# A fused attention and feed-forward layer: latent keys on another engine, and the order of both ends

## The reference

```python
qkv = x @ qkv_w + qkv_b                        # 16 heads of 16
local = windowed_attention(q, k, v)            # each token sees the 128 in front of it
pooled = x.reshape(B, 64, 8, D).mean(axis=2)   # 64 latent tokens
rq = x @ rq_w + rq_b                           # 4 latent heads of 16
rk, rv = split(pooled @ rkv_w + rkv_b)
remote = softmax(mask(rq @ rk.T / 4)) @ rv @ rout_w + rout_b
gate = sigmoid(local @ gl_w + remote @ gr_w)   # per head
x1 = layernorm(x + (gate * local + (1 - gate) * remote) @ out_w + out_b)
h = gelu(ternary(w_up) applied to rmsnorm(x1)) # 256 -> 1024
out = layernorm(x1 + ternary(w_down) applied to rmsnorm(h))
```

## Time and profile before

| | us |
|---|---|
| median of 3 runs (lowest, highest) | 1197.87 (1192.1, 1199.39) |
| the profiled execution: its time | 1195.67 |
| its span, first to last instruction | 1193.9 |
| TensorE busy | 1035.2 (87%) |
| VectorE busy | 930.8 (78%) |
| ScalarE busy | 681.3 (57%) |
| GpSimd busy | 714.8 (60%) |
| TensorE's mean granted clock | 0.965 of full |

### The profile page before, as it was taken

One profiled execution on the slowest core, in us unless ns is written; L12 is line 12 of the kernel. 1 busy time (PEld: TensorE's weight loads), 2 busy tenths in 40 slices (PEclk: granted clock), 3 DMA queues, 4 the chain that ended last, 5 costly groups with the idle time before them and its releaser, 6 DMA issues.

```text
span 1193.9 us, 38039 instructions
## 1 busy us (share of the span) xinstructions
PE 1035.2 (87%) x15776; PEld 661.3 (55%) x15776; DVE 930.8 (78%) x2148; ACT 681.3 (57%) x1043; POOL 714.8 (60%) x890
## 2 busy tenths in 40 slices
PE   4767899898999999898999989898999989896855
PEld 2435556565656556565656656565655556563533
DVE  5567888889887878879788878888887887975545
ACT  3414566565656566565656566665646656563733
POOL 5406556675656566675665656675655567564744
PEclk9977999999999999999999999999999999996977
DMA  6640241606133250605233160604225060511000
GB/s 219 177 130 3 79 119 41 176 23 166 50 109 91 74 143 32 185 23 145 54 114 103 49 169 32 178 29 126 74 80 137 32 186 23 150 29 39 2 19 18
DMA packets 51272, 108.19 MB, mean 91 GB/s; under 512 B 8054, under 2 KB 35190, under 8 KB 47990
## 3 DMA queue, kind: packets, MB, share of 16 engines
q1 hardware_dynamic: 50460, 105.75, 31.5%
q10 hardware_dynamic: 640, 0.00, 0.0%
HBM read 71.55 MB, written 34.08 MB: 88 GB/s over the span
## 4 chain that ended last, share of the span: by engine, by line
PE 46%; DVE 34%; ACT 8%; issue 6%; POOL 5%; ACTq 0%; DVEq 0%; POOLq 0%
PE oacc L1508 7%; PE oacc L1489 7%; PE work L1565 6%; PE work L1432 5%; PE scores L1469 4%; ACT Pt L793 4%; DVE Pt L979 3%; PE work L1499 3%; DVE nmax L1059 3%; DVE stats L1146 2%; DVE Pt L1017 2%; DVE x L1122 2%; DVE ytok L1140 2%; PE scores L1411 2%; POOL h_lo L664 2%
## 5 line engine op out<-in xcount | busy, mean ns | idle before, releaser
L793 ACT ACTIVATE Pt<-scores 128x1024 f32<-128x1024 f32 (+1 forms) x256 | 228.7, 915 | 116.3 <-PE oacc L1489 75.2
L1059 DVE TENSOR_REDUCE nmax<-work 128x3 f32<-128x480 f32 x352 | 218.2, 637 | 29.5 <-PE work L1437 24.2
L664 POOL TENSOR_TENSOR h_lo<-hbuf,h_hi 128x512 f16<-128x512 f32 x128 | 149.2, 1170 | 133.8 <-DVE h_hi L1181 133.8
L636 POOL TENSOR_SCALAR_AFFINE_SELECT Pt<-Pt 128x512 f32<-128x512 f32 x256 | 166.1, 649 | 95.0 <-ACT Pt L793 93.8
L628 POOL TENSOR_TENSOR parts<-Pt,parts 128x512 bf16<-128x512 f32 x64 | 72.4, 1159 | 142.7 <-ACT parts L743 133.0
L1432 PE MATMUL work<-Ks,Qs 98*32 98x160 bf16 x4096 | 142.0, 236 | 15.2 <-DVE nmax L1059 11.5
L1489 PE MATMUL oacc<-Pt,Vp 128*32 128x256 f32 (+1 forms) x2048 | 149.2, 358 | 4.0 <-POOL Pt L640 3.6
L1508 PE MATMUL oacc<-wdn_t,h_hi 128*128 128x256 f16 x512 | 118.1, 273 | 17.4 <-POOL h_lo L664 17.4
L1469 PE MATMUL scores<-Qs,Ks 100*32 100x160 bf16 (+4 forms) x4096 | 113.9, 228 | 18.9 <-ACT Pt L793 15.9
L640 POOL TENSOR_SCALAR_AFFINE_SELECT Pt<-Pt 128x512 f32<-128x512 f32 x192 | 126.7, 660 | 0.0
L829 ACT ACTIVATE hbuf<-work 128x512 f32<-128x512 f32 x128 | 76.2, 595 | 76.7 <-PE work L1565 61.4
(11 more groups left out here) (169 smaller groups left out, 2078.1 us busy)
## 6 DMA issues: line engine op xcount, KB each, us to landing
parts_scratch<-parts SPq DMA_DIRECT2D x96, 256.0 KB, 5.6
Qs<-parts_scratch SPq DMA_DIRECT2D x96, 256.0 KB, 5.0
Ks<-parts_scratch SPq DMA_DIRECT2D x96, 256.0 KB, 4.7
xtok<-L_attn_x SPq DMA_DIRECT2D x16, 512.0 KB, 6.8
xres<-L_attn_x SPq DMA_DIRECT2D x16, 512.0 KB, 7.7
y<-ytok SPq DMA_DIRECT2D x16, 512.0 KB, 3.3
nat<-L_ffn_w_up SPq DMA_DIRECT2D x1, 1024.0 KB, 8.3
nat<-L_ffn_w_down SPq DMA_DIRECT2D x1, 1024.0 KB, 10.3
```

The costliest lines, as they stand in the source:

```text
L636: ins = pool.affine_select(out=pt[:, :, 0:P], in_=pt[:, :, 0:P], compare_op=ALU.is_gt, fill=0.0, base=0, pattern=[[0, 4], [1, P]], channel ...
L664: pool.tensor_tensor(h_lo[:, t % NR, :], hbuf[:, t % 2, :], h_hi[:, t % NR, :], ALU.subtract).then_inc(h_lo_ready, 1)
L793: nc.scalar.activation(Pt[:, u % NPT, :, 0:w], scores[:, slot, :, :].rearrange("p k (h q) -> p (k h) q", h=2)[:, :, 0:w], ACT.Exp, scale=S ...
L1059: nc.vector.tensor_reduce(nmax[:, :, :].rearrange("p b h -> p (b h)")[:, first:first + n], work[:, slot, 0:n * BAND].rearrange("p (h c) -> ...
```

## The change

Eight edits, all in the order of the work or in who does it; the result is the same function.

1. In LAT_RKV ScalarE makes `rqT` and, by four instructions with a scale and a bias for each partition (`lat_fold`), the four blocks of `lat_bd` straight from the accumulator. VectorE's two instructions (`rqT`, `rk_sb`) and GpSimd's product go. VectorE now waits for ScalarE's blocks (`bd_ready`) ahead of `rv_bd`. `lat_fold` is made once (step FOLD).
2. GpSimd's fourth subtraction moves from QK+3 to LAT_RKV, which is behind its OUT, for sequences 2 and on.
3. LAT_NORM moves behind the first step UP.
4. Prologue: FOLD (with ScalarE's share of PREP) goes ahead of QK+3, LAT_SCORES and LAT_EXP of sequence 0 ahead of VALUES, `prepare` behind LAT_RKV; GpSimd's EDGES waits for the fourth subtraction.
5. Prologue, beside the tiles A of sequence 0: LAT_SCORES and LAT_EXP of sequence 1 move in among them, VALUES+2 and VALUES+3 behind them.
6. The first ternary matrix (step TERNARY, both passes) moves into the prologue, ahead of LAT_T of sequence 1.
7. The second one is cut into three pieces at u = 2, 5 and 8, and the intermediate result lies in the target itself.
8. The first three score tiles of sequence 15, with their exponentials, move into the second half of sequence 14, behind GATE; TensorE's wait for the maxima moves to the first score tile. GpSimd's masks stay where they were.

```diff
@@ -75,7 +75,7 @@
     ("F", NORM + 1), ("P", LAT_EXP), ("P", VALUES + 1), ("F", XN_T), ("F", XN_T + 1), ("F", XN_HI),
-    ("P", LAT_EXP + 1), ("F", XN_LO), ("P", VALUES + 2), ("P", LAT_NORM), ("F", UP), ("F", UP + 1),
+    ("P", LAT_EXP + 1), ("F", XN_LO), ("P", VALUES + 2), ("F", UP), ("P", LAT_NORM), ("F", UP + 1),
     ("P", VALUES + 3), ("P", LAT_NORM + 1), ("F", UP + 2), ("F", UP + 3), ("P", LAT_T), ("P", LAT_T + 1),
@@ -94,14 +94,16 @@
 F_RESULTS |= {UP + f: [("F", 6 + f)] for f in range(FT)}
-PREP, EDGES, SUMS, WEIGHTS_T = 0, 1, 2, 3
+FOLD, PREP, EDGES, SUMS, TERNARY, WEIGHTS_T = 0, 1, 2, 3, 4, 5
+AHEAD = 3
 def order_of_attention(i):
-    order = [("S", i, 0)]
+    early = AHEAD if i == B - 1 else 0
+    order = [] if early else [("S", i, 0)]
     for u in range(FIRST_HALF):
-        if u + 1 < NU:
+        if early <= u + 1 < NU:
             order.append(("S", i, u + 1))
@@ -120,6 +122,8 @@
             order.append((phase, i if phase == "F" else i + 2, k))
+        if i == B - 2 and (phase, k) == ("F", GATE):
+            order += [("S", B - 1, u) for u in range(AHEAD)]
         if i == 0 and phase == "P" and QK <= k < QK + 4:
@@ -127,21 +131,21 @@
-    order = [("P", 0, k) for k in (X_T, QK, QK + 1, QK + 2, QK + 3)] + [("W", 0, PREP)]
-    order += [("P", 0, LAT_RQ), ("P", 0, LAT_RKV), ("W", 0, EDGES)]
-    order += [("P", 0, VALUES + b) for b in range(NB)]
-    order += [("P", 0, k) for k in (LAT_SCORES, LAT_EXP, LAT_EXP + 1, LAT_NORM, LAT_NORM + 1)] + [("P", 1, X_T)]
-    order += [("P", 0, LAT_T), ("P", 0, LAT_T + 1)]
+    order = [("P", 0, k) for k in (X_T, QK, QK + 1, QK + 2)] + [("W", 0, FOLD)]
+    order += [("P", 0, k) for k in (QK + 3, LAT_RQ, LAT_RKV)] + [("W", 0, PREP), ("W", 0, EDGES)]
+    order += [("P", 0, k) for k in (LAT_SCORES, LAT_EXP, LAT_EXP + 1, VALUES, VALUES + 1, LAT_NORM, LAT_NORM + 1,
+                                    VALUES + 2, VALUES + 3)]
+    order += [("P", 1, X_T), ("P", 0, LAT_T), ("P", 0, LAT_T + 1)]
     order += [("P", 1, QK + c) for c in range(4)]
     order += [("P", 0, LAT_O), ("P", 1, LAT_RQ), ("P", 1, LAT_RKV), ("W", 0, SUMS)]
-    between = [("P", 0, k) for k in (REMOTE, REMOTE + 1)] + [("P", 1, VALUES + b) for b in range(NB)]
+    between = {1: ("P", 0, REMOTE), 3: ("P", 0, REMOTE + 1), 5: ("P", 1, VALUES), 8: ("P", 1, VALUES + 1),
+               17: ("P", 1, LAT_SCORES), 19: ("P", 1, LAT_EXP), 20: ("P", 1, LAT_EXP + 1)}
     for v in range(NM):
         order.append(("A", 0, v))
-        if v % 2 == 1 and between:
-            order.append(between.pop(0))
+        if v in between:
+            order.append(between[v])
         order += [("T", 0, t) for t in range(2) if v == T_AFTER[t] + 1 or v == T_AFTER[t] == NM - 1]
-    order += between
-    order += [("P", 1, k) for k in (LAT_SCORES, LAT_EXP, LAT_EXP + 1, LAT_NORM, LAT_NORM + 1)]
+    order += [("P", 1, k) for k in (LAT_NORM, LAT_NORM + 1, VALUES + 2, VALUES + 3)] + [("W", 0, TERNARY)]
     return order + [("P", 1, k) for k in (LAT_T, LAT_T + 1, LAT_O, REMOTE, REMOTE + 1)]
@@ -614,19 +617,18 @@
             def p_step(s, k):
-                if k == LAT_RKV:
-                    pool.wait_ge(rk_ready, count(s, 1, 0))
-                    pool.tensor_tensor(lat_bd[:, :, :], rk_sb[:, :].unsqueeze(1).to_broadcast([P, LH, LAT]),
-                                       diag_mask[:, :, :], ALU.mult).then_inc(bd_ready, 1)
-                if QK <= k < QK + 4:
-                    t = k - QK
+                def last_parts(t):
                     pool.wait_ge(part1, count(s, 4, t))
                     if t == 0 and not s.first:
                         pool.wait_ge(parts_out, count(s, 2, -1) * 48)
                     pool.tensor_tensor(parts[:, 2, t, :], qk_rest[:, t, :], parts[:, 1, t, :],
                                        ALU.subtract).then_inc(part2, 1)
+                if QK <= k < QK + 4 and (s.i < 2 or k < QK + 3):
+                    last_parts(k - QK)
+                if k == LAT_RKV and s.i >= 2:
+                    last_parts(3)
@@ -741,6 +743,20 @@
                         nc.scalar.activation(parts[:, 1, t, :], qk_rest[:, t, :], ACT.Copy).then_inc(part1, 1)
+                if k == LAT_RKV:
+                    bank, n = p_use(s, R_RQ)
+                    act.wait_ge(p_full[bank], n + 1)
+                    nc.scalar.activation(rqT[:, :], p_bank(bank)[:, 0:S // 2], ACT.Identity, bias=brq[:, :]
+                                         ).then_inc(p_taken[bank], 1)
+                    if s.first:
+                        act.wait_ge(fold_ready, 1)
+                    bank, n = p_use(s, R_RKV)
+                    act.wait_ge(p_full[bank], n + 1)
+                    for h in range(LH):
+                        ins = nc.scalar.activation(lat_bd[:, h, :], p_bank(bank)[:, 0:LAT], ACT.Identity,
+                                                   scale=lat_fold[:, 0, h:h + 1], bias=lat_fold[:, 1, h:h + 1])
+                    ins.then_inc(bd_ready, 1)
                 if LAT_EXP <= k < LAT_EXP + 2:
@@ -838,7 +854,7 @@
                 for u in range(FIRST_HALF):
-                    if u < NU:
+                    if u < NU and not (s.last and u < AHEAD):
                         weights(s, u)
@@ -853,11 +869,14 @@
                         p_step(later, k)
+                    if s.i == B - 2 and (phase, k) == ("F", GATE):
+                        for u in range(AHEAD):
+                            weights(s.next(), u)
                     if s.first and phase == "P" and QK <= k < QK + 4:
                         w_step(WEIGHTS_T + k - QK)
             def w_step(j):
-                if j == PREP:
+                if j == FOLD:
                     act.wait_ge(w_in, W_ALL)
@@ -937,19 +956,40 @@
+                if j == FOLD:
+                    dve.wait_ge(w_in, W_ALL)
+                    dve.wait_ge(consts, 2)
+                    nc.vector.tensor_scalar(lat_fold[:, 0, :], diag[:, :], 1.0 / CHUNK, None, ALU.mult)
+                    nc.vector.tensor_scalar(lat_fold[:, 1, :], diag[:, :], brk[:, :], None, ALU.mult
+                                            ).then_inc(fold_ready, 1)
                 if j == PREP:
                     prepare()
-            def ternary_weights(k):
-                if k == 0:
+                if j == TERNARY:
                     dve.wait_ge(alpha_all, 1)
                     nc.vector.tensor_scalar(alpha[:, 0:2], alpha[:, 4:6], 0.5 / (F * D), None, ALU.mult)
                     link(nc.vector.tensor_scalar(alpha[:, 6:8], alpha[:, 4:6], -0.5 / (F * D), None, ALU.mult))
-                link(nc.vector.tensor_scalar(below, nat[k], alpha[:, 6 + k:7 + k], None, ALU.is_lt))
-                nc.vector.scalar_tensor_tensor(out=ternary[k], in0=nat[k], scalar=alpha[:, k:k + 1],
-                                               in1=below, op0=ALU.is_gt, op1=ALU.subtract
-                                               ).then_inc(tern, 1)
-                dve.wait_ge(tern, k + 1)
+                    below(0)
+                    above(0, slice(0, F * D // P)).then_inc(tern, 1)
+            def below(k):
+                link(nc.vector.tensor_scalar(ternary[k], nat[k], alpha[:, 6 + k:7 + k], None, ALU.is_lt))
+            def above(k, cols):
+                return nc.vector.scalar_tensor_tensor(out=ternary[k][:, cols], in0=nat[k][:, cols],
+                                                      scalar=alpha[:, k:k + 1], in1=ternary[k][:, cols],
+                                                      op0=ALU.is_gt, op1=ALU.subtract)
+            def ternary_down(part):
+                half = F * D // P // 2
+                if part == 0:
+                    below(1)
+                if part == 1:
+                    above(1, slice(0, half))
+                if part == 2:
+                    above(1, slice(half, 2 * half)).then_inc(tern, 1)
@@ -989,21 +1029,16 @@
                 if k == LAT_RKV:
-                    bank, n = take(R_RQ)
-                    nc.vector.tensor_scalar(rqT[:, :], p_bank(bank)[:, 0:S // 2], brq[:, :], None, ALU.add
-                                            ).then_inc(p_taken[bank], 1)
                     bank, n = take(R_RKV)
+                    dve.wait_ge(bd_ready, count(s, 1, 0))
                     for i in range(2):
                         rows = slice(i * LD, (i + 1) * LD)
                         of_head = p_bank(bank)[rows, LAT:LAT + LD].rearrange("p (t h d) -> p t h d", t=2, h=2)
                         bias = brv[rows, :].rearrange("p (t h d) -> p t h d", t=2, h=2)
-                        nc.vector.scalar_tensor_tensor(out=rv_bd[rows, :, i * LHD:(i + 1) * LHD],
-                                                       in0=of_head[:, :, i, :], scalar=1.0 / CHUNK,
-                                                       in1=bias[:, :, i, :], op0=ALU.mult, op1=ALU.add)
-                    nc.vector.tensor_scalar(rk_sb[:, :], p_bank(bank)[:, 0:LAT], 1.0 / CHUNK, brk[:, :],
```

(15 more changed lines are left out.)

24 lines of the change are left out of this document (10 added, 14 removed).

## The result

In the comparison the changed kernel takes 1160.03 us (median of 4 runs, 1155.59 to 1161.29), the kernel before 1196.67 (4 runs, 1192.1 to 1199.39): a ratio of 0.9691, 95% interval 0.965 to 0.9732. The forecast was 1166, with a range of 1150 to 1180. The profiled execution of the changed kernel has a span of 1158.3 us and a mean granted clock of 0.965, the same clock as before.

What follows compares the result with a forecast made beforehand. VectorE's chain was taken to bound second halves and mostly the prologue, TensorE the first half and feed-forward. Gains 16.8 + 4.5 + 8 + 0 + 0.9 = 30.2 us off 1195.67 gave 1165.5, stated as 1166, range 1150 to 1180.

Steps and rivals of the forecast that it cites:

- the periods: Second halves of sequences 0 to 13: each period 1.2 us shorter (0.6 to 1.8), 16.8 us over 14.
- The copy behind GpSimd: VectorE's copy of line 1151 waits 0.81 us for GpSimd's subtractions; with three ahead it costs 0.17 instead of 0.98.
- Keys on ScalarE: VectorE's chain in LAT_RKV saves 0.39 and 0.43 us and newly waits 0.4 for ScalarE's four blocks of 0.37 each.
- LAT_NORM behind the first UP: Second half, feed-forward start: moving LAT_NORM's 1.7 us gains nearly nothing beyond the shift; taken as 0, bounds 0 and 0.5.
- Prologue: Up to the first score tile, edits 4 to 6: gain 4.7 us, taken as 4.5 (0 to 7).
- First half of sequence 0: Ternary work moved out and cut into pieces: 4.3 + 2 + 1.7 = 8 us gained (5 to 10), leaving 26.
- End: Sequences 14 and 15: score tiles moved ahead are free, 0 for TensorE's clock, 0.9 us gained at sequence 15's start.
- A: Rival: ScalarE wait of 0.9 and the moved subtraction meeting the copy leave the period 0.5 gain; 1175 us, chance 0.15.
- B: Rival: blocks take 0.256, edit 3 adds 0.2, the clock comes up; 1.8 per period, 1150 us, chance 0.13.
- C: Rival, prologue: `prepare` waits beside GpSimd's writes and 4.5 us of gain are lost; 1170 us, chance 0.07.
- D: Rival: slower, ScalarE's keys late in every second half; decisive above 2.6 us of wait, 1215 at 4 us, chance 0.03.

Runs made afterwards that it cites:

- e5: Changed kernel with edit 1 undone: VectorE makes rqT and rk_sb again, GpSimd the latent key blocks; 1161.99 us, ratio to the kernel before 0.9695 to 0.9728.
- e3: Changed kernel with edit 3 undone: LAT_NORM again ahead of the first step UP; 1164.45 us, ratio to the kernel before 0.9719 to 0.9748.
- e10: Changed kernel, but VectorE and GpSimd make the latent keys of sequences 0 and 1, ScalarE those of 2 to 15; 1152.59 us.
- e1: Changed kernel with edit 8 undone: the three score tiles back at the start of sequence 15; 1153.37 us, ratio to the kernel before 0.9633 to 0.9666.
- e9: Changed kernel with edit 7's cut undone: the three pieces of the second ternary matrix stand together at u = 8; 1164.66 us.
- e2: Changed kernel plus one small exponential on ScalarE behind sequence 14's last gelu, drawing the table load forward; 1157.62 us.
- e4: Changed kernel with edit 2 undone: all four GpSimd subtractions again in QK to QK+3; 1165.00 us, ratio to the kernel before 0.972 to 0.976.

## Why the prediction was right, step by step

The time is within the range, 6 us below the forecast; the direction held in each stretch but the last. Part of that is luck: the periods gave 8 us more than forecast and the end 3 less, and the prologue's sum came out right over parts that did not.

- **The copy behind GpSimd (edit 2)**: right. 0.81 was a wait, and it is gone; alone the edit is worth 0.55, because the copy's stall had covered the wait for ScalarE.
- **Keys on ScalarE (edit 1)**: the mechanism is right, the wait was mis-sized: 0.28 where 0.4 stood. Four blocks take 1.28, 0.32 each, between the bound of 0.256 and the 0.37 taken from the pointer row. By the figures of the Trainium skill, "ScalarE: Activation LUTs", section "What ACT_TABLE_LOAD costs", the estimate is 0.33 for one of them behind another and 1.42 for four; the trace has 1.28. The rule of the same page, section "Rules for kernel authors", that such arithmetic belongs on VectorE does not decide a kernel in which VectorE is on the chain: e5 measures 0.51 per period in favour of ScalarE.
- **LAT_NORM behind the first UP (edit 3)**: the step that failed. It was counted as 0, with a bound of 0.5; e3 measures 0.33, 4.6 us over 14 periods. The argument was that LAT_NORM still stands ahead of the second `h_hi`. That is so, and TensorE's fourth UP does wait for that sum; but the wait ends 0.36 sooner than the one it replaces, for GpSimd's first `h_lo`. The first `h_hi` comes 0.8 earlier (1.93 us behind the table load of the gelus instead of 2.73), and 0.33 of that lasts to the end of the period, with a shorter LAT_NORM+1 beside it.
- Together: 0.81 + 0.39 + 0.43 - 0.28 = 1.35 at `ytok` (in the two profiles `ytok` stands 13.41 and 12.09 us behind its gate, 1.32 apart), and 0.33 make 1.68; the period shrank by 1.65. The prediction had 1.2. This is 6 us of the 8 by which the periods were undercounted; the other 2 are the first period and the single longer ones.
- **Prologue**: the sum of prologue and first half was right (12.8 for 12.5) and its parts were not: luck. To LAT_T 4.2 (4.0). The loss at ScalarE's keys of sequence 1 came, 1.9 where 2.2 stood (from VectorE's first operation on the projections to the first maxima 10.05 us instead of 8.18); in e10, without it, LAT_T and the first maxima are 1.5 closer. But TensorE's clock, which the prediction left at its old level ahead of the tiles and did not question among them, gave 1.5 between LAT_T and the projections (LAT_T takes 1.06 instead of 1.97), so that 3.8 are left at the first maxima where 1.8 stood. The tiles last 24.1 us where 19.5 stood. Of these 4.6, 1.2 are VectorE's wait behind the latent scores, taken as 0.5 (1.67 in e10, which needs 20.7 us), and 3.3 go with the lower clock, 2.6 of them in the difference to e1. Then 10.6 instead of 11.9 to the first score tile. The prologue alone gained 3.5 where 4.5 stood.
- **First half of sequence 0 (edits 6 and 7)**: 28.3 us to the gate instead of 37.6, a gain of 9.3 where 8 was forecast. The price of an undivided block was taken as 2 + 1.7; e9 measures 4.0.
- **End (edit 8)**: the sign failed. Forecast was a gain of 0.9, with 0 for the clock; the profiles have a loss of 2.2. "Free" was said of where the tiles go, and nothing of the place they leave. There they filled TensorE's wait for `ytok`, and ScalarE's table load leaned on them; e2 shows that the load is the larger part.
- **Rivals**: A (VectorE's time given back) is refuted in the period by e5 and e4, and describes the prologue well, where the wait is 2.59. B (all of it counts) named edit 3's 0.2 and was nearer there, and nearer on the period (1.8 for a measured 1.65); on the wait it was not: it had none, and 0.28 is nearer to the forecast's 0.4. C: `prepare` ran beside GpSimd's writes at its old pace, 0.42 to 0.43 an operation, in a window in which GpSimd is busy 4.77 of 5 us:

```profile
26.90 0.43 DVE L950 TENSOR_TENSOR ytok<-bv,glb 128x256 f32<-128x256 f32 x1
```

```profile
25.00:30.00 5.00, 3.14 (x13) 1.77 (x14) 4.63 (x12) 0.00 (x0) 4.77 (x5) 0.50 0.60 166
```

  The contention that the Trainium skill states for two SBUF inputs ("GPSIMD Engine Reference", "Key points") does not show beside a write that reads nothing; it does at LAT_NORM+1, whose product has two SBUF inputs and lies beside a subtraction (1.22, 1.44 and 2.03 us, e3). D did not occur; the wait is 0.28 of the 2.6 it needed.

## What to carry to other kernels

When work is moved forward, ask not only whether its new place is free but what it covered in its old one: here a table load on ScalarE, which came onto the path and cost 1.6 to 2.6 us, and a wait of 2.7 us on TensorE. An edit that is good in the steady state can be bad in the prologue, where the engine that takes the work over is not idle; making it depend on the sequence number gave 8 us. And a new wait of 2 us on TensorE can cost more than 2 us: here the clock was lower behind it, and the tiles took 3.3 us longer.

## What the runs showed of the hardware

- **One prologue, two courses.** The same instructions gave first score tiles at 82.6 and 85.9 (e1 and changed kernel), with the granted clock at 1.00 and at 0.50 between 65 and 70 us; 0.4 of the 3.3 us between them is older than that (LAT_T at 37.22 and 37.60).
- **A table load stands where its first user waits.** In the changed kernel it starts at 1087.24, 7.04 us after ScalarE's last work, not at its beginning; in e1 it follows the gelu at once. It takes 1.28 us in both, and the next exponential starts at 1088.54, 0.02 behind it. The Trainium skill, "ScalarE: Activation LUTs", section "What ACT_TABLE_LOAD costs", adds 1.38 us of draining to each load; neither place shows that.
- **VectorE is held by some of GpSimd's work and not by other.** VectorE's copy of 128x2 elements takes 0.98 until GpSimd's subtraction ends, and 0.17 otherwise. The cast `h_hi` takes 0.43, and 1.01 where it starts 0.44 us into a subtraction (608.13, changed kernel). The product of LAT_NORM+1 takes 1.22 alone and up to 2.03. The `prepare` operations lost nothing beside GpSimd's fills.
- **It can be GpSimd that is held.** In e3, at 1007.08, in the last second half that has steps P, the same product takes 1.22 beside two subtractions, and these take 3.44 us instead of 2.38.
